# ScalarE instead of SyncE issues the transfers that shift the values by 64 tokens

## What is computed

```python
x = L0_attn_x                                     # (8, 512, 256)
xn = _layernorm(x, axis=-1)
# attention: window of 64 keys for each query
q, k, v = (split_heads(xn @ W) for W in (Wq, Wk, Wv))
k_win, v_win = take(k, idx), take(v, idx)         # idx = l - 63 ... l
attn = softmax(where(invalid, -inf, einsum('bhld,bhlwd->bhlw', q, k_win) * scale))
ctx = einsum('bhlw,bhlwd->bhld', attn, v_win)
# feed-forward: absmean(W) is W made ternary
h = gelu(einsum('btd,hd->bth', xn, absmean(W_fc)))
h = layernorm(h, ln_w, ln_b)
out = x + ctx @ Wo + einsum('bth,dh->btd', h, absmean(W_proj))
```

## Time and profile before

| | |
|---|---|
| median of 3 runs | 487.81 us (485.13 to 488.44) |
| the profiled execution | 487.92 us, of it 486.0 us span |
| PE busy | 413.5 us (85%) |
| DVE busy | 348.1 us (72%) |
| ACT busy | 308.7 us (64%) |
| POOL busy | 187.3 us (39%) |
| mean granted clock of PE | 0.94 |
| DMA packets of the one hardware queue | 33.56 MB, 43.2% of 16 engines |

### The profile page before, as it was taken

How to read it: one execution, slowest core, us unless ns; L and a number is a source line. 1 busy time by engine, 2 the same in 40 slices (tenths; PEclk the granted TensorE clock), 3 DMA queues, 4 the chain that set the end, 5 groups by cost and what they waited for, 6 DMA issues and landing times.

```text
span 486.0 us, 13187 instructions
## 1 busy us (share of the span) xinstructions
PE 413.5 (85%) x5644; PEld 273.3 (56%) x5644; DVE 348.1 (72%) x692; ACT 308.7 (64%) x393; POOL 187.3 (39%) x113
## 2 busy tenths in 40 slices
PE   0269298999979999799979999899979998999885
PEld 0143065477636775377536774577537763676563
DVE  1967077869964987298955987398748995598663
ACT  2305246789566868487647868586748856786460
POOL 7400100456323534056314634155505721364551
PEclk9999679999998999799988999899979999999797
DMA  7805903930394018900592029800790029502001
GB/s 257 186 1 78 96 1 90 136 36 3 98 138 49 25 41 138 105 3 24 127 129 27 24 63 134 87 13 27 149 119 4 24 59 131 50 24 53 15 23 45
DMA packets 35226, 34.41 MB, mean 71 GB/s; under 512 B 5152, under 2 KB 33824, under 8 KB 35168
## 3 DMA queue, kind: packets, MB, share of 16 engines
q1 hardware_dynamic: 35168, 33.56, 43.2%
HBM read 7.35 MB, written 4.19 MB: 24 GB/s over the span
## 4 chain that ended last, share of the span: by engine, by line
PE 50%; DVE 20%; DMA 10%; SPq 9%; issue 6%; ACT 4%; POOL 1%; POOLq 0%; ACTq 0%
DMA v_odd<-v_even 8%; PE big L1040 7%; SPq L323 7%; PE small L1107 6%; PE small L1096 6%; DVE y_bufs L758 5%; PE small L1123 4%; PE big L1026 4%; PE big L1014 4%; DVE negmax L722 4%; PE big L1086 4%; PE big L1074 3%; DVE g_lo L716 2%; PE big L1079 2%; PE big L1059 2%
## 5 line engine op out<-in xcount | busy, mean ns | idle before, releaser
L455 POOL TENSOR_TENSOR p_parts<-probs,p_parts 128x1024 f16<-128x1024 f32 x64 | 137.3, 2152 | 174.2 <-ACT p_parts L573 174.2
L572 ACT ACTIVATE probs<-big,exp_scale 128x1024 f32<-128x1024 f32 x64 | 71.6, 1119 | 35.8 <-PE big L1079 35.4
L722 DVE TENSOR_REDUCE negmax<-big 128x8 f32<-128x1024 f32 x64 | 77.8, 1219 | 19.4 <-PE big L1059 18.7
L573 ACT ACTIVATE p_parts<-big,exp_scale 128x1024 f16<-128x1024 f32 x64 | 71.5, 1117 | 0.0
L550 ACT ACTIVATE gel<-big 128x1024 f32<-128x1024 f32 x32 | 32.7, 1022 | 43.9 <-PE big L1040 43.8
L1096 PE MATMUL small<-proj_t,g_hi 128*128 128x256 f16 x256 | 58.6, 277 | 0.0
L1096 PE MATMUL small<-proj_t,g_lo 128*128 128x256 f16 x256 | 58.3, 276 | 0.0
L1040 PE MATMUL big<-fc_t,xt_hi 128*128 128x512 f16 x128 | 54.3, 424 | 1.4 <-DVE fc_t L845 0.9
L1040 PE MATMUL big<-fc_t,xt_lo 128*128 128x512 f16 x128 | 54.5, 425 | 0.0
L587 ACT ACTIVATE g_hi<-big,lnw_s 128x512 f16<-128x512 f32 x64 | 40.5, 692 | 17.5 <-PE big L1086 17.0
L716 DVE SCALAR_TENSOR_TENSOR g_lo<-big,lnw_s,g_hi 128x512 f16<-128x512 f32 x64 | 44.8, 743 | 2.1 <-ACT g_hi L587 1.7
(11 more groups left out here) (130 smaller groups left out, 816.7 us busy)
## 6 DMA issues: line engine op xcount, KB each, us to landing
q_stack<-qk_split SPq DMA_DIRECT2D x64, 128.0 KB, 5.0
k_stack<-qk_split SPq DMA_DIRECT2D x64, 128.0 KB, 7.8
x_in<-in_x SPq DMA_DIRECT2D x8, 512.0 KB, 3.9
out<-y_bufs SPq DMA_DIRECT2D x32, 128.0 KB, 1.7
v_odd<-v_even SPq DMA_DIRECT2D x16, 132.0 KB, 2.6
v_odd<-v_even SPq DMA_DIRECT2D x16, 99.0 KB, 2.6
gel<-in_w_fc SPq DMA_DIRECT2D x1, 1024.0 KB, 6.3
y_bufs<-in_w_proj SPq DMA_DIRECT2D x1, 1024.0 KB, 9.1
```

The source lines that it names most:

```text
L455: g.tensor_tensor(p_lo[:, j % PB], probs[:, j % PB], p_hi[:, j % PB], ALU.subtract).then_inc(*sig(p_lo_ready))
L572: s.activation(probs[:, j % PB].rearrange("p i (u q) -> p u i q", u=2), st, ACT.Exp, scale=exp_scale[:, 0:1]).then_inc(*sig(exp_ready))
L573: s.activation(p_hi[:, j % PB].rearrange("p i (u q) -> p u i q", u=2), st, ACT.Exp, scale=exp_scale[:, 0:1]).then_inc(*sig(p_hi_ready))
L722: v.tensor_reduce(negmax[:, j], slot[b, "sa", j][:].rearrange("p a (u k) -> p (a u) k", k=P), AX.X, ALU.max, negate=True).then_inc(*sig(ma ...
```

## The change

`shift_values` moves from SP's program into ACT's. It waits for the same two semaphores and issues the same two transfers for each part; their destinations, sources and the semaphore that counts the landings stay. On SP its calls disappear. On ACT the two calls stand at new places: part 0 behind `qk_upper(p + 1, 0)`, part 1 behind `exp(p, 1)`. A transfer that ACT issues goes through ACT's own queue. All else is unchanged, except that all lines behind L325 move (L328 and L329 are now L535 and L536).

```diff
@@ block.sync
             @per_batch
-            def shift_values(b, part):
-                wait(sp, b, (v_hi_ready, v_ready)[part], 1)
-                sp.dma_start(v_odd[0:W, part, 1:NT], v_even[W:P, part, 0:NT - 1]).then_inc(*sig(v_shifted))
-                sp.dma_start(v_odd[W:P, part], v_even[0:W, part]).then_inc(*sig(v_shifted))
...
             for p in range(NB + 3):
                 store(p + 1, 1)
                 load_stack(p + 3, 0, 0)
                 load_stack(p + 3, 0, 1)
-                shift_values(p + 2, 1)
                 load_stack(p + 3, 1, 0)
                 load_stack(p + 3, 1, 1)
                 load_shift(p + 2, 1)
                 store(p + 1, 2)
                 store(p + 1, 3)
                 load_shift(p + 3, 0)
                 store(p + 2, 0)
-                shift_values(p + 3, 0)
                 load_x(p + 5)
@@ block.scalar
+            @per_batch
+            def shift_values(b, part):
+                wait(act, b, (v_hi_ready, v_ready)[part], 1)
+                act.dma_start(v_odd[0:W, part, 1:NT], v_even[W:P, part, 0:NT - 1]).then_inc(*sig(v_shifted))
+                act.dma_start(v_odd[W:P, part], v_even[0:W, part]).then_inc(*sig(v_shifted))
...
                 xt_upper(p + 1)
                 v_upper(p)
                 qk_upper(p + 1, 0)
+                shift_values(p, 0)
                 exp(p, 0)
                 exp(p, 1)
+                shift_values(p, 1)
                 gelu(p + 1, 0)
                 qk_upper(p + 1, 1)
```

More of the change, by code:

```diff
@@ L325, in shift_values @@
             @per_batch
-            def shift_values(b, part):
-                wait(sp, b, (v_hi_ready, v_ready)[part], 1)
-                sp.dma_start(v_odd[0:W, part, 1:NT], v_even[W:P, part, 0:NT - 1]).then_inc(*sig(v_shifted))
-                sp.dma_start(v_odd[W:P, part], v_even[0:W, part]).then_inc(*sig(v_shifted))
-            @per_batch
             def load_shift(b, h):
@@ L378, in _ @@
             load_shift(0, 0)
-            shift_values(0, 0)
             load_x(2)
@@ L382, in _ @@
             load_stack(1, 0, 1)
-            shift_values(0, 1)
             load_stack(1, 1, 0)
@@ L388, in _ @@
             store(0, 0)
-            shift_values(1, 0)
             load_x(3)
@@ L393, in _ @@
             load_stack(2, 0, 1)
-            shift_values(1, 1)
             load_stack(2, 1, 0)
@@ L401, in _ @@
             store(1, 0)
-            shift_values(2, 0)
             load_x(4)
```

## The result

The changed kernel takes 489.06 us (median of 20 executions, 486.38 to 491.38), the kernel before 486.59 us (20 executions beside it, 481.03 to 491.89): a ratio of 1.0076, with an interval of 1.0048 to 1.0103. The change makes the kernel slower, by 0.5 to 0.8%, where 0.9% faster was forecast. Its profiled execution took 488.54 us, of it 486.6 us span.

The account below looks back on a forecast made before the run. PE's wait before pv, with the stacks' landing close behind, was taken as the bound. Six periods of 1.49 + 0.6 - 2.01 + 0.70 = 0.78 us give 4.7, less 0.5: 487.92 to 483.7 us; range 471 to 493.

Parts of the forecast that it names:

- What bounds the kernel now: PE waits before pv for v_odd, 2.75 us in six batches; a second wait, for the stacks, is hidden behind it.
- the slack behind it: Between PE's readiness for sa and the last k_stack landing: mean 1.63 us, of which 1.49 us a period is usable.
- What is late next: Before sa of the next batch: PE gains 4.76 us, uses 1.49, and stands 3.27 us waiting for the stacks.
- Do the stacks land earlier?: Stack transfers without values in their ring: last landing 0.6 us earlier a period, bounds 0 and 1.9; skill's rule says 0.
- at most 1.9 us belong to the two value transfers: Of the 17.6 us from first to last stack landing, the upper bound on the value transfers' share.
- What the moved wait costs: Behind sa, PE's clock falls after the moved wait: 2.01 us lost a period, bounds 0 and 2.49.
- DVE's catching up: While PE stands before sa, DVE catches up, shortening g_lo waits: 0.70 us regained a period, bounds 0 and 1.0.
- it needs no correction: The profiled execution of 487.92 us taken as the base, since the median of the runs was 487.81.
- nothing is left: Rival: stacks land as before; slack and DVE just pay for the clock, 487 to 488 us; chance 0.23 with its variant.
- slower: Rival: PE loses 2.49 us a period behind sa and nothing is given back, 494.4 us; chance 0.18.
- ACT's cost: The moved issues on ACT, 2.5 us a batch: cost nothing while a pair adds less than about 2 us.
- The ends: Batch 0: nothing; batch 7: part 1 lands at most 1.5 us late behind exp(7, 1), costing 0.5 us.

Follow-up runs that it names:

- Experiments 9: Changed kernel with each of the sixteen stack transfers copying only half its tokens from batch 2 on (a bound, not a gain): 458.93 us, 0.9454.
- 12: Kernel before, with part 1 issued early from SP, stack halves in turn, and the store behind the first four q_stack issues: 458.42 us, 0.9476.
- experiments 3: Kernel before, all on SP, with part 1 of the values issued directly behind load_x, ahead of the stack transfers: 475.39 us, 0.9775.
- experiment 7: Changed kernel with ACT issuing part 1 directly behind part 0, ahead of both exponentials and of the stack transfers: 474.96 us, 0.9774.
- experiment 4: The kernel before, run once more unchanged to show how much its own traces differ: 484.95 us, 0.9989.
- experiment 2: Kernel before with only part 0 of the values moved to ACT, part 1 kept on SP: 483.86 us, 0.9847.
- experiment 1: Kernel before with only part 1 of the values moved to ACT, part 0 kept on SP: 488.14 us, 1.0101.
- experiment 6: Kernel before with 8 matmuls of constants filling PE's wait before pv in the six periods: 479.88 us, 0.9861.
- experiment 11: Changed kernel with SP's store of an output tile moved behind the first four q_stack issues, so the stacks start earlier: 464.01 us, 0.9595.

## Why the prediction was wrong

**What bounds the kernel now: right.** The wait before `pv` vanished, and the slack behind it, 1.63 us on average, was what could be used. `sa` follows the last landing by 0.14 us, as taken. Experiments 9 and 12 show that nothing else stands close behind.

**What is late next: right.** A wait of 3.27 us was forecast in six periods; the six waits are 20.8 us together, 3.5 each.

**Do the stacks land earlier? Wrong.** "I take 0.6 us" was the first step that failed. The burst is 21.58 us in place of 21.33, 0.25 more and not 0.6 less, though single values of either kernel scatter by 0.7 to 1.1 us. The bound "at most 1.9 us belong to the two value transfers" was sound: in the last five periods experiments 3 and 7 got 1.2 and 1.3 of them (20.26 and 20.12 us against 21.42). But only by moving them out of the burst. In the changed kernel ACT issues part 1 just behind the second q_stack issue, right into it. The Trainium skill's rule (page "DMA: Bandwidth & Descriptors", section "Issuing engines are not separate DMA queues"), by which transfers from all issuing engines interleave on the same DMA engines, gave 0 for this term, and the trace, with its -0.25, agrees that nothing is gained. The error is 0.85 us a period, 5.1 us in all.

**What the moved wait costs: right for the changed kernel, wrong for the one before.** The price of 2.01 us behind `sa` measured 1.93, DVE's catching up 0.75 (0.70 was taken). What failed is the sentence "Each wait before `pv` therefore costs 2.75 us of standing still and 2.01 us of slow running". It was read from one execution, in which the clock fell in all six periods. That execution had a mean clock of 0.940 where the kernel's mean is 0.952, and its 487.92 us are 1.3 above the 486.59 of the twenty, so "it needs no correction", which rested on three runs, failed too. Half speed for a share of 1 - 0.952 = 0.048 of the clock means 0.096 of the span, 46.6 us; the changed kernel has 55.6 us. These 9 us at half clock are worth up to 4.5 us of PE's time, more than the 2.5 us by which the medians differ. Trading six waits that cost the clock much of the time (five of six in experiment 4, one of six in experiment 2) for six that cost it nearly always (six of six in the profile, five in experiment 1) was a loss that the sum had at nothing. The rival "nothing is left" (487 to 488) came nearest in mechanism; the rival "slower" had the right sign by the clock, but priced it at 2.49 us in place of counting how often it is paid.

**ACT's cost: right.** The issues run beside the activations, and no PE wait of over 0.7 us for ACT is in the six periods. The cover is real too: experiment 7's 1.45 us of standing still cost nothing there.

**The ends.** In batch 7 a wait of 1.9 us for v_odd appeared (1.5 was the bound), as ACT reaches part 1 only behind `exp(7, 1)`. Yet from the third `gt` of batch 7 on the changed trace is 1.4 us shorter and not 0.5 longer: its clock is at 0.50 for 10.7 us there, against 15.2 before. The profiled execution also began 2.4 us later (`sa(0, 0)` at 63.08 in place of 60.63) before any moved transfer was issued. In the kernels that leave the moved transfers on SP it is 61.61 (experiment 4) and 63.27 (experiment 6) as well, so that belongs to the execution and not to the change.

In sum the six periods of the two traces, each with its wait and the slow running behind it (from the third `gt` of batch 1 to that of batch 7), take 317.8 and 317.3 us: 0.5 us in favour of the change, where 4.7 were forecast. The 4.2 us between are the stacks' 5.1, less some 0.8 by which the clock and DVE came out better than taken. So in this pair the first failed step is the whole error of the periods. The medians, over all the clock's patterns, turn the sign; that part is the second.

Open: what decides whether a given wait lowers the clock. Lengths from 1.6 to 3.2 us did both (1.61 us in experiment 11 lowered it, 1.62 in experiment 2 didn't).

## What to carry to other kernels

Before a wait is removed, read off how far behind it the next transfer's landing lies: here 1.6 of 4.8 us could be gained, and the rest moved to the next job. When a queue of transfers is the bound, a small transfer in its midst costs its share from any queue; issue it before the burst begins, and begin the burst as early as its first input allows. Where the granted clock falls behind waits, one profiled execution is one draw: compare its mean clock with those of the other executions before a price is read from it. Several short waits may be better than one long one: in experiment 7 the clock held behind them.

## What was unexpected of the hardware

- PE's clock falls behind waits of 1.8 us (to 0.50 for 3.4 us) and holds behind others of 3.1 and 3.2 us, in executions of nearly the same program. The mean clock of one kernel went from 0.937 to 0.971 and its time from 477.6 to 492.0 us.
- Matmuls of constants in place of 2.6 us of each of six idle times made the kernel 2% faster, from 489.06 to 479.14 us.
- Two transfers in a queue of their own took 4.1 and 6.8 us to land beside a burst in the other queue, against 5.3 and 6.5 us in the same queue: the second gained nothing, and ahead of a burst (experiment 7) it took 2.5.
- ACT's sequencer issues a transfer within 0.01 us of starting an activation; two issues (0.47 and 0.61 us) hide behind it almost wholly, four don't.
